# Probability strips of a context-attention loop through DRAM in halves: eight writes and two reads per pair of blocks in place of four and one

## The reference

```
Q_char = x_n @ Wq_c.T + bq_c           # x_n: layernorm of x, 256 x 512
K_sub  = ctx @ Wk_s.T + bk_s           # ctx: 25088 x 512
V_sub  = ctx @ Wv_s.T + bv_s
scores = Q_char @ K_sub.T / sqrt(512)
char2sub = softmax(scores) @ V_sub
```

## Time and profile before

| | us |
|---|---|
| median of 3 runs | 1169.48 |
| lowest and highest of them | 1167.11 and 1169.86 |
| the profiled execution, its own time | 1165.06 |
| its span in the profile | 1163.3 |

### The profile page before, as it was taken

The page is one execution under the profiler, slowest core; times in us unless marked ns, Lnnn a source line. Parts: engine busy times, 40 slices in busy tenths (PEclk is TensorE's granted clock), DMA queues, the critical chain, the costliest instruction groups (busy, mean ns, idle before and its releaser), DMA issues.

```text
span 1163.3 us, 16777 instructions
## 1 busy us (share of the span) xinstructions
PE 1038.4 (89%) x6736; PEld 714.6 (61%) x6736; DVE 618.1 (53%) x977; ACT 372.8 (32%) x546; POOL 3.5 (0%) x20
## 2 busy tenths in 40 slices
PE   9999999999999999999999999999887666667666
PEld 8867878878888888888866756454432222222223
DVE  4457878878878878878854365222121111111112
ACT  2444456546546556546433252000000000000000
POOL 1000000000000000000000000000000000000000
PEclk9999999999999999999999999999997898997989
DMA  9548799887888887888859435999999999999997
GB/s 347 188 145 301 284 350 349 305 297 282 286 296 284 285 303 278 286 298 282 287 193 384 145 145 230 428 425 425 426 426 426 428 428 428 428 428 429 426 429 308
DMA packets 91122, 381.48 MB, mean 328 GB/s; under 512 B 5584, under 2 KB 6224, under 8 KB 74064
## 3 DMA queue, kind: packets, MB, share of 16 engines
q1 hardware_dynamic: 91088, 381.00, 84.1%
HBM read 355.29 MB, written 25.69 MB: 327 GB/s over the span
## 4 chain that ended last, share of the span: by engine, by line
DMA 47%; PE 27%; DVE 17%; SPq 4%; ACT 2%; issue 2%; DVEq 0%; ACTq 0%
DMA deep<-in_r_down 23%; DMA strips<-turned 11%; DMA pt<-strips 9%; DVE nat_lo L1261 4%; DVE turned L1288 4%; PE ps L984 4%; DVE pt_lo L1266 4%; SPq L351 3%; DMA wide<-in_r_up 3%; DVE st L1273 2%; ACT pt_hi L1052 2%; PE ps L544 2%; PE ps L970 2%; PE ps L964 1%; DMA nat<-in_ctx_rows 1%
## 5 line engine op out<-in xcount | busy, mean ns | idle before, releaser
L558 PE MATMUL ps<-ctt_hi,q_hi 128*128 128x512 f32 x392 | 153.7, 392 | 0.0
L560 PE MATMUL ps<-ctt_hi,q_lo 128*128 128x512 f32 x392 | 152.6, 389 | 0.0
L559 PE MATMUL ps<-ctt_lo,q_hi 128*128 128x512 f32 x392 | 152.5, 389 | 0.0
L571 PE MATMUL ps<-nat_hi,pt_hi 128*128 128x512 f32 x368 | 143.8, 391 | 3.9 <-DVE pt_lo L1266 3.9
L573 PE MATMUL ps<-nat_hi,pt_lo 128*128 128x512 f32 x368 | 143.3, 389 | 0.0
L572 PE MATMUL ps<-nat_lo,pt_hi 128*128 128x512 f32 x368 | 143.3, 389 | 0.0
L1205 ACT ACTIVATE sg<-ps 128x256 f32<-128x256 f32 x32 | 12.3, 384 | 388.0 <-PE ps L964 388.0
L1602 DVE TENSOR_TENSOR hh<-sg,ps 128x256 f32<-128x256 f32 x32 | 13.5, 421 | 227.7 <-PE ps L970 227.7
L984 PE MATMUL ps<-deep,hh_t 128*32 128x512 f32 x496 | 77.9, 756 | 54.9 <-DMA deep<-in_r_down 53.6
L1256 DVE TENSOR_TENSOR ctt_lo<-ctt,ctt_hi 128x2048 fp32r<-128x2048 f32 x49 | 111.0, 2289 | 18.6 <-ACT ctt_hi L1044 18.2
L1048 ACT ACTIVATE nat_hi<-nat 128x2048 fp32r<-128x2048 f32 x48 | 92.1, 1918 | 79.4 <-DMA nat<-in_ctx_rows 79.4
(11 more groups left out here) (281 smaller groups left out, 1257.4 us busy)
## 6 DMA issues: line engine op xcount, KB each, us to landing
wide<-in_r_gate SPq DMA_DIRECT2D x32, 2048.0 KB, 26.0
wide<-in_r_up SPq DMA_DIRECT2D x32, 2048.0 KB, 27.4
deep<-in_r_down SPq DMA_DIRECT2D x31, 2048.0 KB, 25.8
ctt<-in_ctx_t SPq DMA_DIRECT2D x49, 1024.0 KB, 7.9
nat<-in_ctx_rows SPq DMA_DIRECT2D x48, 1024.0 KB, 7.4
strips<-turned SPq DMA_DIRECT2D x96, 256.0 KB, 5.1
pt<-strips SPq DMA_DIRECT2D x24, 1024.0 KB, 4.8
w_gate<-in_w_g_t SPq DMA_DIRECT2D x2, 1024.0 KB, 13.6
```

The lines of the kernel that those rows point to most:

```text
L558: mm(o, qh, ctt_hi[par][:, c, :], start=(c == 0), stop=False)
L559: mm(o, qh, ctt_lo[par][:, c, :], start=False, stop=False)
L560: last = mm(o, ql, ctt_hi[par][:, c, :], start=False, stop=(c == HC - 1))
L571: mm(o, p_hi[:, w, :], n_hi[:, t, :], start=(first and t == 0), stop=False)
```

## The change

The strips go out and come back by half. `spread` waits for the turn of one half, issues four writes of that half (128 KB each, runs of 1 KB where they were 2 KB), then waits for the turn of the other half and issues its four writes. A new function `gather_strips` behind it waits for the writes of one half and issues a read of that half (512 KB, 4 KB for each partition where it was 8 KB), then does so for the other half. `pt` and `strips` are laid out with the half ahead of the group. Each half has semaphores of its own, and `pt_hi` of a half waits for that half's read only. `turned` keeps its layout. The bytes moved are the same.

```
-        pt = at("pt", [P, G, 2, QT * KT, Q], F32, LOOPB + 10 * kb)
+        pt = at("pt", [P, 2, G, QT * KT, Q], F32, LOOPB + 10 * kb)
...
-        strips = nc.dram_tensor("strips", (P, G, 2 * QT * KT * Q), F32, kind="Internal").ap()
+        strips = nc.dram_tensor("strips", (P, 2, G, QT * KT * Q), F32, kind="Internal").ap()
...
             def spread(u):
-                sp.wait_ge(s["turned_ready"], u * 2 + 2)
-                for g in range(G):
-                    sp.dma_start(strips.rearrange("(k j) g n -> j k g n", k=G)[:, :, g, :],
-                                 turned[g * Q:(g + 1) * Q, :, :, :, :].rearrange("j k h w i -> j k (h w i)")
-                                 ).then_inc(s["strips_stored"], 16)
-                sp.wait_ge(s["strips_stored"], u * (16 * G) + 16 * G)
-                sp.dma_start(pt[:, :, :, :, :].rearrange("p g h w i -> p (g h w i)"), strips.rearrange("p g n -> p (g n)")
-                             ).then_inc(s["pt_loaded"], 16)
+                for half in range(2):
+                    sp.wait_ge(s["turned_ready"], u * 2 + 1 + half)
+                    for g in range(G):
+                        sp.dma_start(strips.rearrange("(k j) h g n -> j k h g n", k=G)[:, :, half, g, :],
+                                     turned[g * Q:(g + 1) * Q, :, half, :, :].rearrange("j k w i -> j k (w i)")
+                                     ).then_inc(strips_stored[half], 16)
+
+            def gather_strips(u):
+
+                for half in range(2):
+                    sp.wait_ge(strips_stored[half], u * (16 * G) + 16 * G)
+                    sp.dma_start(pt[:, half, :, :, :].rearrange("p g w i -> p (g w i)"),
+                                 strips[:, half, :, :].rearrange("p g n -> p (g n)")).then_inc(pt_loaded[half], 16)
...
                 spread(u)
+                gather_strips(u)
...
             def probs_hi(u, half):
-                act.wait_ge(s["pt_loaded"], u * 16 + 16)
+                act.wait_ge(pt_loaded[half], u * 16 + 16)
                 act.activation(pt_hi[:, half, :, :].rearrange("p w (g i) -> p w g i", g=G),
-                               pt[:, :, half, :, :].rearrange("p g w i -> p w g i"), ACT.Copy).then_inc(s["pt_hi_ready"], 1)
+                               pt[:, half, :, :, :].rearrange("p g w i -> p w g i"), ACT.Copy).then_inc(s["pt_hi_ready"], 1)
```

More of the change, by code:

```diff
@@ L234, in perceiver_layer @@
         x_loaded0 x_loaded1 cols_loaded rows_loaded wqc_loaded wks_loaded wkc_loaded wqs_loaded wvc_loaded sel_loaded
-        wg2_loaded wg1_loaded wvs_loaded nat_loaded0 nat_loaded1 ctt_loaded0 ctt_loaded1 end_nat_loaded strips_stored pt_loaded watt_loaded wo_loaded
+        wg2_loaded wg1_loaded wvs_loaded nat_loaded0 nat_loaded1 ctt_loaded0 ctt_loaded1 end_nat_loaded strips_stored0 strips_stored1 pt_loaded0 pt_loaded1 watt_loaded wo_loaded
         gsh_loaded ush_loaded dsh_loaded
@@ L260, in perceiver_layer @@
         ctt_loaded = [s["ctt_loaded0"], s["ctt_loaded1"]]
+        strips_stored = [s["strips_stored0"], s["strips_stored1"]]
+        pt_loaded = [s["pt_loaded0"], s["pt_loaded1"]]
         tile_loaded = [s["tile_loaded0"], s["tile_loaded1"], s["tile_loaded2"], s["tile_loaded3"],
@@ L386, in _ @@
             spread(0)
+            gather_strips(0)
             half = HC // 2 * DA
@@ L1266, in probs_lo @@
                 dve.tensor_tensor(pt_lo[:, half, :, :].rearrange("p w (g i) -> p w g i", g=G),
-                                  pt[:, :, half, :, :].rearrange("p g w i -> p w g i"),
+                                  pt[:, half, :, :, :].rearrange("p g w i -> p w g i"),
                                   pt_hi[:, half, :, :].rearrange("p w (g i) -> p w g i", g=G).bitcast(F32),
```

## The result

The changed kernel is slower, by 1.3%: 1182.35 us (1178.44 to 1185.47) against 1168.3 us (1163.46 to 1169.86), median of 4 runs each; the ratio is 1.0129, with a 95% interval of 1.0099 to 1.016. The forecast was 1164.4 us, faster; 1182 lies outside its range.

The account below looks back on a forecast made before the run. The prediction took PE to bound the loop, with 5.1 us of waits to win. Its terms, -3.9 in early pairs, 0 in 260 to 560 us and -1.2 behind the loop, took 1169.5 to 1164.4 us; range 1161.5 to 1172.

Parts of the forecast that it names:

- What bounds the kernel: In the loop PE's own work sets the pace; its idle time, 5.1 us, is all the change can take.
- The terms of -3.9 and -1.2: PE's waits for `pt_lo` vanish: 3.9 us in the early pairs, 1.2 us behind the loop.
- In 260 to 560 us: 0: Middle stretch of the loop, where PE is always busy: the change neither gains nor loses time.
- the ring: Chain beside PE's work: turn, strip write, read, `pt_hi`, `pt_lo`, exponentials, next turn; about as long as PE's 21.75 us pair.
- The spare of the second ring: The chain from turn to next turn was taken to have some 0.35 us to spare in each pair against PE.
- The margin of 0.8 us: In the ordinary pair, `pt_lo` of half 0 ends some 0.8 us before PE reaches the products.
- Half 0: First half's strips: written 1.06 us sooner, read back 2.3 us earlier, its `pt_lo` ending 2.0 us earlier.
- The read of half 1: Second half's read lands 3.3 us after issue, so this half is there 0.9 us earlier.
- The writes: Eight strip writes in place of four: the last landing of a pair comes 0.6 us later.
- `nat[1]`: the sign: Load of rows queued behind the reads: taken to land 0.9 us earlier, over the alternative of 0.6 us later.
- The first rival: The wait moves to `nat[1]`, giving back 3 to 5 us: no change, 1167.5 to 1170 us; chance 0.22.
- The slow rival: Runs of 1 KB make strip writes land 2.6 us later; PE waits, 17 us slower, 1187 us; chance 0.12.

Follow-up runs that it names:

- e15: Kernel before, each strip write cut in two by half: eight writes in 1 KB runs behind both turns, one read; 1174.62 us, ratio 1.0063.
- e14: Kernel before, each strip write cut in two by target rows: eight writes in 2 KB runs behind both turns, one read; 1176.41 us, ratio 1.0061.
- e2: Changed kernel with its eight writes, but one read of 1 MB behind all of them; 1181.26 us, ratio 1.0123 to the kernel before.
- e9: Kernel before, fourth strip write left out from the second pair on; 1309.78 us, ratio 1.1220, though the loop ended 3.7 us earlier.
- e1: Changed kernel with the halves apart in DRAM, each half's read one contiguous 512 KB; 1174.85 us, ratio 1.0050 to the kernel before.
- e12: Changed kernel with halves contiguous in DRAM and both reads behind all eight writes; 1179.10 us, ratio 1.0096 to the kernel before.
- e8: Changed kernel, but neither read issued before all eight writes have landed; 1182.91 us, ratio 1.0116 to the kernel before.
- e3: Kernel before, its 1 MB read cut into two of 512 KB in 4 KB pieces 8 KB apart, after all four writes; 1185.16 us, ratio 1.0138.
- e13: Kernel before, its read cut in two by partitions, 64 partitions of 8 KB each; 1219.12 us, ratio 1.0443.
- e5: Kernel before, load of `nat[0]` moved from ahead of the four strip writes to behind them; 1236.37 us, ratio 1.0578.
- e6: Changed kernel, load of `nat[0]` moved from ahead of the eight strip writes to behind them; 1191.45 us, ratio 1.0184 to the kernel before.

## Why the prediction was wrong

**What bounds the kernel: right.** No idle PE in 260 to 560 us, 5.1 us to win and no more. So any error could only be a loss, and the prediction did not draw this conclusion.

**The terms of -3.9 and -1.2: right by themselves.** No wait for `pt_lo` is left in front of the first products of a pair, as was forecast. What failed is the term "In 260 to 560 us: 0". There PE lost 36 matmuls, 8.2 us, to new waits in front of the products of half 1; with the early pairs and the end of the loop these waits are more than what was won. The term rested on two steps, that `nat[1]` would come 0.9 us earlier and that the ring had spare if it didn't.

**The spare of the second ring: the step that failed first.** The prediction took "a spare of some 0.35 us" from the exponentials of one pair, 21.4 us after those of the pair before. In the pair right behind it the turns are 22.3 us apart, and the mean of 15 pairs is 21.76, PE's own time. The row that would have told it is DVE's, in the timeline of the kernel before:

```profile
327.19 1.22 DVE L1273 TENSOR_REDUCE st<-ps 128x2 f32<-128x1024 f32 x1
```

This maximum of half 1 starts directly behind `pt_lo` of half 1 and doesn't wait for PE's scores, and so it is in all of the 13 pairs from 260 to 560 us, while the maximum of half 0 does wait for PE, 0.2 to 0.7 us. In steady state PE and the ring were level. What holds them level the trace only suggests: `nat[0]`, which SP issues when PE's products release it, goes ahead of the strips in the queue, and the later it is issued after the turn, the longer the pair (1.30 us: 22.29; 0.78 us: 21.62; over the 15 pairs the correlation is 0.81). No run tests this alone. The margin of 0.8 us ahead of PE's products, also in the prediction, is a buffer that is used up once, not a spare in each pair. The runs on the writes alone show the price: in e15, e14 and e2 the last read was issued 0.19, 0.30 and 0.46 us later, and the cycle was 0.23, 0.34 and 0.50 us longer. With 22 pairs, 0.1 us later costs 2 us and more. That earlier gains nothing is argued from the same picture; e9 agrees with it.

**Half 0: right, and worth nothing.** It was to come 2.3 us earlier; `pt_hi` of half 0 starts at 11.72 in place of 14.20 us after the turn, 2.5 earlier. The ring does not pass through it: `pt_lo` of half 1 and `nat[1]` close it.

**The read of half 1: mis-sized.** Forecast 3.3 us from issue to landing. The line of the reads has (min/median/max):

```profile
DMA to landing us min/median/max: 3.6/4.7/7.2
```

`pt_hi` of half 1 starts at 15.19; in the kernel before it started at 15.17, but there a full microsecond behind the landing, after that of half 0. So the half lands 0.9 us later, not 0.9 earlier. The runs gave two parts: the pieces' place in DRAM (e1, and e12 against e8), and the writes still under way beside the first read (e8). Where neither is there, in e12, two reads were through as fast as one.

**The writes: too large, and priced at nothing.** I had the last landing 0.6 us late. In e14 and e15, where only the writes are changed, it is 0.2 to 0.3, in e2 0.46. In the changed kernel itself the last read, which waits for this landing, is issued 0.4 us nearer to the turn than before (8.99 for 9.38); but there `nat[0]`, too, is issued nearer to the turn (0.16 us behind it for 1.00). The half's 1.3 us on the queue and the 2.6 us of all strips don't follow from the 328 GB/s beside them, by which they are 1.6 and 3.2. The term was in the prediction, and the sum gave it nothing because the spare and the faster read were to swallow it.

**`nat[1]`: the sign was wrong.** I chose 0.9 us earlier, by the bytes ahead of it, over 0.6 later, by today's time from its issue. It came 0.67 us later (18.07 for 17.40), although it was issued 0.4 earlier. The first rival named this wait and its place in the ring, and priced it as "no change", again because of the spare.

**The slow rival** had the right side and total (17 us) by the wrong mechanism: 1 KB runs cost nothing of their own (e14 against e15). The rule of the Trainium skill that stood beside it, that a DMA wants 1 MB or more to reach 75% of the peak ("DMA: Bandwidth & Descriptors", section "Bandwidth"), agrees with the trace for a single DMA: a read of 512 KB in e12 landed in 3.9 us (median), one of 1 MB before in 4.8. It doesn't carry over to two reads issued one behind the other, which overlap: in e12 both were through in 4.6 us. The 0.6 us more in e3 came from the places of the pieces.

**What stays open.** Why `nat[1]` takes 8.4 us in e12 with the reads ahead of it done early. This is the wait that closes the ring in e12, so the loss that is left there, 1.0096 in time, is placed but not explained.

None of the sixteen runs beat the kernel before.

## What to carry to other kernels

Where one engine is busy for all of a loop, look for the second ring beside it, and take its spare from the mean over many turns and from the instruction where the ring waits for the busy engine: if it never waits there, take it that there is no spare and that a change can only lose, until a run shows otherwise. Splitting a transfer brings the first part earlier and the last part later; ask which of the two the ring passes through. And cost the transfer that is queued behind: here it was the load behind the split reads that set the new cycle.

## What the runs showed of the hardware

- A read to half of the partitions is slow: two reads of 512 KB with 64 partitions and 8 KB pieces landed in 5.9 us (median) each, while one read of 1 MB over 128 partitions took 4.8. One pair of e13, and its 7.93 us of waiting:

```profile
361.06 1.09 SPq L356 DMA_DIRECT2D pt<-strips  x2
...
367.97 2.00 ACT L1053 ACTIVATE pt_hi<-pt 128x1024 fp32r<-128x1024 f32 x2 [7.93 <-DMA pt<-strips]
```

- Four writes of 256 KB, each from 32 partitions, took as long alone (230 GB/s with the head of the next load) as beside a load of 1 MB (328 GB/s together). Taking the load away from in front of them gained nothing (e5). Eight writes of 128 KB did gain by it: their last landing came 1.5 us earlier (e6).
- Pieces of 4 KB that lie 8 KB apart in DRAM were read slower than the same pieces side by side: the median of a 512 KB read was 4.7 us in the changed kernel and 3.9 in e1. With both reads behind all writes, 1 MB took 5.5 us (e8) and 4.6 (e12) from the first issue to the last landing; as one read it took 4.8.
- A load of 1 MB behind two such reads landed later even where the reads were through sooner: 8.4 us from its issue in e12, 7.5 before.
- "issue" as releaser can hide a wait for an engine: here it stood for `nat_lo`, which ended 0.10 us before the matmul started in each of the ten waits.
